# Row halves transposed by DMA for a first FFN layer, and a new timetable of branch steps between gate products

## The reference

```python
x = x + jnp.tanh(g_xattn[0]) * wkv0(w, u, k=_layernorm(x), v=ctx)
x = x + jnp.tanh(g_ffn[0]) * ffn0(_layernorm(x))
x = x + jnp.tanh(g_xattn[1]) * wkv1(decay, first, k=_layernorm(x), v=ctx)
x = x + jnp.tanh(g_ffn[1]) * moe(_layernorm(x))
# ffn0: hidden = silu(x @ W1.T) * (x @ W3.T), 2048 wide; hidden = fwht(hidden); out = hidden @ W2.T
# wkv: y_t = (sum over s < t of decay * exp(k_s) v_s + exp(u + k_t) v_t) / (the same without v)
# moe: 8 experts of width 1024, two of them per row, silu(x @ w1.T) * (x @ w3.T) @ w2.T
```

## Time and profile before

| what | us |
|---|---|
| median of three runs (lowest, highest) | 1480.47 (1476.39, 1480.92) |
| the profiled execution | 1483.66 |
| its span | 1482.0 |
| PE busy in the span | 1244.8 (84%) |
| DVE busy | 726.9 (49%) |
| ACT busy | 504.1 (34%) |
| POOL busy | 201.2 (14%) |
| mean granted clock of PE | 0.935 |

### The profile page before, as it was taken

The page is one execution under the profiler, slowest core; times in us unless marked ns, Lnnn a source line. Parts: engine busy times, 40 slices in busy tenths (PEclk is TensorE's granted clock), DMA queues, the critical chain, the costliest instruction groups (busy, mean ns, idle before and its releaser), DMA issues. The chain is left out here.

```text
span 1482.0 us, 18672 instructions
## 1 busy us (share of the span) xinstructions
PE 1244.8 (84%) x5785; PEld 590.9 (40%) x5786; DVE 726.9 (49%) x1175; ACT 504.1 (34%) x671; POOL 201.2 (14%) x206
## 2 busy tenths in 40 slices
PE   1278899898998898988913199989999999999995
PEld 0143344444453344534413044434444444444442
DVE  6957966869677686795675211212122122221221
ACT  3337557476563665645432011111111111111110
POOL 0000000000002000030200413222222223222222
PEclk9989999999999999999955599999999999999998
DMA  6024576554756556637776278798959896955433
GB/s 253 29 114 136 178 248 220 171 191 171 254 166 85 181 197 219 214 95 260 213 204 208 46 182 160 146 121 179 186 138 189 178 201 134 163 120 100 77 67 61
DMA packets 228347, 239.13 MB, mean 161 GB/s; under 512 B 137168, under 2 KB 141520, under 8 KB 225168
## 3 DMA queue, kind: packets, MB, share of 16 engines
q1 hardware_dynamic: 84960, 164.58, 36.3%
q10 hardware_dynamic: 130368, 51.65, 20.4%
q0 software_dynamic: 12960, 22.15, 7.8%
...
## 5 line engine op out<-in xcount | busy, mean ns | idle before, releaser
L1084 PE MATMUL PS<-weights,xs 128*128 x1872 | 412.9, 381 | 29.5 <-DMA xs<-X 29.5
L1009 PE MATMUL PS<-xs,weights 128*128 128x512 f16 x1536 | 358.4, 390 | 26.8 <-DVE sg L845 15.1
L1084 PEld LDWEIGHTS PS<-weights,xs 128*128 128x128 f16 x1872 | 183.8, 98 | 252.3 <-issue 33.3
L1009 PEld LDWEIGHTS PS<-xs,weights 128*128 128x128 f16 x1536 | 152.6, 100 | 222.9 <-issue 24.2
L912 DVE SCALAR_TENSOR_TENSOR A<-A,PS 128x1024 f32<-128x1024 f32 x39 | 47.6, 1221 | 352.2 <-PE PS L1084 324.1
L1021 PE MATMUL PS<-weights,hs 128*128 128x512 f16 x768 | 181.3, 387 | 0.0
L604 ACT ACTIVATE A<-PS 128x1024 f32<-128x1024 f32 x39 | 39.9, 1024 | 320.1 <-PE PS L1084 192.2
...
L923 DVE TENSOR_SCALAR V<-PS,outl 128x512 f32<-128x512 f32 x39 | 29.3, 751 | 166.7 <-PE PS L1098 150.6
L1021 PEld LDWEIGHTS PS<-weights,hs 128*128 128x128 f16 x768 | 76.4, 100 | 86.2 <-issue 6.6
L1098 PE MATMUL PS<-weights,xs 128*128 x456 | 104.0, 386 | 7.9 <-DMA weights<-e 4.6
L612 ACT ACTIVATE E<-A 128x1024 f16<-128x1024 f32 x39 | 41.2, 1056 | 198.6 <-DVE A L912 156.0
...
## 6 DMA issues: line engine op xcount, KB each, us to landing
e<-halves SPq DMA_DIRECT2D x192, 256.0 KB
...
raw<-ew SPq DMA_DIRECT2D x119, 256.0 KB, 4.0
...
V<-ctx_cm ACTq DMA_DIRECT2D x7, 1024.0 KB, 5.7
X<-w ACTq DMA_DIRECT2D x4, 1024.0 KB, 6.1
out<-X ACTq DMA_DIRECT2D x4, 1024.0 KB, 9.9
...
```

The lines of the kernel that those rows point to most:

```text
L1009: ins = te.matmul(bank(bk), wj[:, j, w, a, c * P:(c + 1) * P], xs[:, g % 2, b, c, :], start=(k == 0 and c == 0), stop=(k == 2 and c == C - 1))
L1084: ins = te.matmul(bank(n), xTt[k][:, b, c, :], weights_of(off, 2 * I // NT * c + n, a), start=(c == 0 and m == 0), stop=(c == C - 1 and m ...
```

## The change

- STEPS has four places: ACT's and DVE's chunks are written anew. Place 2 is on ACT behind hh, place 3 on ACT and DVE at the chunk's end. DVE runs only places 0 and 3, ACT all; PE places 0 and 1 as before. Unit 0 stands behind silu on ACT and behind the gate product on DVE, all other units behind hh and place 2 (ACT) and behind hl (DVE). The residual moves from the head of chunk j = 1 to behind hl of chunk j = 0.
- In STEPS, exp, ln, norm and r2 are at place 2, the scans and the mix at place 3; yT0 is two chunks behind the mix's number. The branches' FIRST, GATES, UNITS and LATE have new numbers.
- The pre branches of groups 1 to 3 have no xT0 and xT1. xh copies the second norm's rows to the high half in `xr` (ACT), xl makes the low half (DVE), and the step xd issues four transposing DMAs from ACT, one per tile of 128 rows (128 x 1024 of float16), from `xr` into `xs`. PE waits for them (xs_in) at j = 0, and so does k0 ahead of its scans, since SQ is their source. Pre 0 in the prologue keeps its PE transposes.
- The bonus on the key sums moves from k1 and den into k0 and k1, and all scans of V into den.

```diff
 ADD, SUB, MUL, MAXO = ALU.add, ALU.subtract, ALU.mult, ALU.max
 
 
-UNITS = [[3, 3, 3, 3, 0, 3, 3, 3, 2, 3, 3, 3, 4, 4, 4, 2],
-         [3, 3, 3, 2, 4, 4, 4, 4, 2, 3, 4, 3, 2, 3, 3, 3],
-         [1, 1, 2, 1, 4, 3, 2, 4, 4, 4, 4, 2, 3, 4, 3, 2],
-         [4, 4, 4, 1, 4, 2, 0, 4, 3, 2, 4, 4, 4, 4, 4, 4]]
+UNITS = [[1, 2, 2, 3, 0, 1, 3, 3, 3, 1, 4, 4, 4, 3, 3, 4],
+         [3, 4, 4, 1, 4, 4, 4, 3, 3, 4, 4, 3, 3, 0, 3, 3],
+         [2, 3, 3, 4, 0, 4, 4, 1, 4, 4, 4, 3, 3, 4, 4, 4],
+         [0, 0, 4, 4, 4, 3, 3, 4, 0, 4, 4, 4, 4, 4, 4, 4]]
 assert sum(map(sum, UNITS)) == NU
 
 
 
-STEPS = [("stats", 0, 0), ("r0", 0, 0), ("newton", 0, 0), ("norm", 1, 0), ("kT0", 1, 1), ("e0", 2, 0), ("k0", 2, 0),
-         ("kT1", 2, 1), ("e1", 3, 0), ("k1", 3, 0), ("den", 4, 0), ("ln", 4, 1), ("rec", 4, 1), ("num", 5, 0), ("mix", 6, 0),
-         ("yT0", 6, 1), ("add0", 7, 0), ("yT1", 7, 1), ("add1", 8, 0), ("r2", 8, 0), ("newton2", 8, 0), ("norm2", 8, 1),
-         ("xT0", 9, 0), ("xh0", 9, 0), ("xl0", 9, 0), ("xT1", 9, 1), ("xh1", 10, 0), ("xl1", 10, 0), ("last", 10, 1),
-         ("raw", 11, 0)]
+
+
+STEPS = [("stats", 0, 0), ("r0", 0, 3), ("newton", 1, 0), ("norm", 1, 2), ("kT0", 2, 1), ("e0", 2, 2), ("k0", 2, 3),
+         ("kT1", 3, 1), ("e1", 3, 2), ("k1", 3, 3), ("ln", 4, 2), ("den", 4, 3), ("rec", 4, 3), ("num", 5, 3), ("mix", 6, 3),
+         ("yT0", 8, 0), ("add0", 8, 0), ("yT1", 8, 1), ("add1", 9, 0), ("r2", 9, 2), ("newton2", 9, 3), ("norm2", 10, 1),
...
+        "post": [("xT0", 11, 0), ("kt0", 11, 0), ("xl", 11, 0), ("xT1", 11, 1), ("kt1", 11, 2), ("last", 12, 0), ("raw", 12, 0)]}
+
+EARLY = {"stats": (1, 0), "r0": (1, 1), "newton": (1, 3), "norm": (1, 3)}
 BRANCHES = [("pre", 0), ("pre", 1), ("pre", 2), ("post", 0), ("pre", 3), ("post", 1), ("post", 2), ("post", 3)]
-FIRST = {("pre", 1): 0, ("pre", 2): 11, ("post", 0): 20, ("pre", 3): 30, ("post", 1): 39, ("post", 2): 49}
-GATE_STEPS = [("gate1", 0), ("gate1b", 0), ("gate2", 0), ("rank", 1), ("ranked", 0)]
-GATES = {0: (31, 32, 34, 34, 35), 1: (50, 51, 53, 53, 54), 2: (60, 61, 62, 61, 62)}
+FIRST = {("pre", 1): -1, ("pre", 2): 9, ("post", 0): 19, ("pre", 3): 29, ("post", 1): 39, ("post", 2): 49}
+GATE_STEPS = [("gate1", 0), ("gate1b", 0), ("rank", 1), ("gate2", 0), ("ranked", 0)]
...
             "xl1", ("h", 3)]
 QORDER = [u for k, u in (x for x in PROLOGUE if isinstance(x, tuple)) if k == "q"]
 
-LATE = {1: 2, 2: 3, 4: 4, 7: 5, 9: 6, 10: 7}
-EPILOGUE = [("post", NG - 1, s) for s, _, _ in STEPS] + [("post", NG - 1, s) for s, _ in GATE_STEPS]
...
+    return sum(kind == "pre" and g > 0 for kind, g in BRANCHES[:b])
 
...
         half = lambda t, a: t[:, :].rearrange("p (c a t) -> p c a t", c=C, t=T)[:, :, a, :]
-        xr = SQ[:, :].bitcast(F16).rearrange("p (s i d) -> p s i d", s=2, i=TILES)
+        xr = SQ[:, :].bitcast(F16).rearrange("p (i s d) -> p i s d", i=TILES, s=2)
...
                     if not second and b >= 1:
-                        act.wait_ge(s["side_full"], FILLS.index(BRANCHES[b - 1] + ("xT1",)) + 1)
-                        act.wait_ge(s["xrl_done"], posts_before(b))
+                        if BRANCHES[b - 1] + ("xT1",) in FILLS:
+                            act.wait_ge(s["side_full"], FILLS.index(BRANCHES[b - 1] + ("xT1",)) + 1)
+                        if b >= 2:
+                            act.wait_ge(s["xrl_done"], b - 1)
...
+                elif step == "xh":
+                    act.wait_ge(s["norm_done"], n + 2)
+                    act.activation(xr[:, :, 0, :], four(A1[:, :]), ACT.Copy, scale=SX).then_inc(s["xrh_done"], 1)
+                elif step == "xd":
+
+                    act.wait_ge(s["xrh_done"], b)
+                    act.wait_ge(s["xrl_done"], b)
+                    if g >= 2:
+                        act.wait_ge(s["b_done"], J * (g - 1))
+                    for i in range(TILES):
+                        act.dma_start_transpose(xs[:, g % 2, :, :, i * P:(i + 1) * P].rearrange("p s c n -> p (s c) n"),
+                                                xr[:, i, :, :].rearrange("p s d -> p (s d)")).then_inc(s["xs_in"], 16)
-                    if kind == "pre":
-                        if a == 0 and g >= 2:
-                            act.wait_ge(s["b_done"], J * (g - 1))
-                        act.activation(xs[:, g % 2, 0, a:a + 2, :].rearrange("p c n -> p (c n)"), side, ACT.Copy, scale=SX).then_inc(s["xh_done"], 1)
-                    else:
-                        act.activation(ch(E1, a, 2), side, ACT.Copy).then_inc(s["kt_done"], 1)
-                        if a == 0:
-                            act.activation(xr[:, 0, :, :].rearrange("p i d -> p (i d)"), A1[:, :], ACT.Copy, scale=SX).then_inc(s["xrh_done"], 1)
-                        else:
-                            rows = xn_rows[g * NT:(g + 1) * NT, :].rearrange("(i p) (s d) -> s p i d", p=P, s=2)
-                            act.wait_ge(s["xrh_done"], g + 1)
-                            act.dma_start(rows[0], xr[:, 0, :, :]).then_inc(s["xn_out"], 16)
-                            act.wait_ge(s["xrl_done"], g + 1)
-                            act.dma_start(rows[1], xr[:, 1, :, :]).then_inc(s["xn_out"], 16)
+                    act.activation(xs[:, 0, 0, a:a + 2, :].rearrange("p c n -> p (c n)"), side, ACT.Copy, scale=SX).then_inc(s["xh_done"], 1)
+                elif step in ("kt0", "kt1"):
+                    a = 2 * int(step[2])
+                    act.wait_ge(s["side_full"], FILLS.index((kind, g, "xT" + step[2])) + 1)
+                    act.activation(ch(E1, a, 2), side, ACT.Copy).then_inc(s["kt_done"], 1)
+                    if a:
+                        rows = xn_rows[g * NT:(g + 1) * NT, :].rearrange("(i p) (s d) -> s p i d", p=P, s=2)
+                        act.wait_ge(s["xrh_done"], b)
+                        act.dma_start(rows[0], xr[:, :, 0, :]).then_inc(s["xn_out"], 16)
+                        act.wait_ge(s["xrl_done"], b)
+                        act.dma_start(rows[1], xr[:, :, 1, :]).then_inc(s["xn_out"], 16)
...
-                for u in units[0:1]:
-                    unit_high(u)
                 if n >= 2:
                     act.wait_ge(s["hl_done"], n - 1)
                 act.wait_ge(s["a_done"], n + 1)
                 act.activation(sg[:, n % 2, :], bank(ABANK), ACT.Silu, scale=1.0 / (SW * SX)).then_inc(s["sil1_done"], 1)
+                for u in units[0:1]:
+                    unit_high(u)
                 for step in steps_beside(g, j, 1):
                     run(*step)
-                for u in units[1:2]:
-                    unit_high(u)
                 if n >= 2:
                     act.wait_ge(s["down_done"], n - 1)
                 act.wait_ge(s["hid_done"], n + 1)
                 act.activation(hs[:, n % 2, 0, :], sg[:, n % 2, :], ACT.Copy).then_inc(s["hh_done"], 1)
-                for u in units[2:]:
+                for step in steps_beside(g, j, 2):
+                    run(*step)
+                for u in units[1:]:
                     unit_high(u)
+                for step in steps_beside(g, j, 3):
+                    run(*step)
...
+                    if pres_before(b):
+                        ve.wait_ge(s["xs_in"], 16 * TILES * pres_before(b))
                     scan(layer, SQ, E1, (0, 1))
+                    bonus(layer, E1, SQ, (0, 1))
                 elif step == "k1":
                     ve.wait_ge(s["e1_done"], 2 * b + 2)
                     link(ve.tensor_tensor(ch(V, 2, 2), ch(E1, 2, 2), ch(V, 2, 2), MUL))
                     scan(layer, SQ, E1, (2, 3))
-                    bonus(layer, E1, SQ, (0, 1))
+                    bonus(layer, E1, SQ, (2, 3)).then_inc(s["den_done"], 1)
                 elif step == "den":
-                    bonus(layer, E1, SQ, (2, 3)).then_inc(s["den_done"], 1)
-                    scan(layer, A1, V, (0, 1, 2))
+                    scan(layer, A1, V, range(C))
                 elif step == "num":
-                    scan(layer, A1, V, (3,))
...
+                elif step == "xl":
+                    ve.wait_ge(s["xrh_done"], b)
+                    ve.scalar_tensor_tensor(xr[:, :, 1, :], four(A1[:, :]), SX, xr[:, :, 0, :], MUL, SUB).then_inc(s["xrl_done"], 1)
...
-                for step in steps_beside(g, j, 0) + steps_beside(g, j, 1):
+                for step in steps_beside(g, j, 0):
                     run(*step)
                 if n in LATE:
                     w_low(LATE[n])
-                for u in units[0:1]:
-                    unit_low(u)
                 ve.wait_ge(s["sil1_done"], n + 1)
                 ve.wait_ge(s["b_done"], n + 1)
                 ve.scalar_tensor_tensor(sg[:, n % 2, :], sg[:, n % 2, :], SH / (SW * SX), bank(BBANK), MUL, MUL).then_inc(s["hid_done"], 1)
-                for u in units[1:2]:
+                for u in units[0:1]:
                     unit_low(u)
                 ve.wait_ge(s["hh_done"], n + 1)
```

(12 more changed lines are left out.)

27 lines of the change are left out of this document (14 added, 13 removed).

## The result

| | before | changed |
|---|---|---|
| median of 10 runs (lowest, highest), us | 1477.17 (1471.82, 1480.92) | 1485.35 (1482.6, 1489.69) |
| ratio, 95% interval | | 1.0059 [1.004, 1.0077] |
| the profiled execution, its span | 1483.66, 1482.0 | 1485.73, 1484.1 |
| first A product, end of the last down product | 113.3, 743.1 | 110.0, 752.0 |
| first stage between them | 629.8 | 642.0 |

The changed kernel is slower by 0.59%, 8.7 us on the median of before; the forecast was +7.5. The profiled spans differ by less, 2.1 us, because the experts' stage took 633.1 us in before's trace and 626.3 in this one; of that, one wait of PE for weights, 4.56 us at 996 us, is in before's trace alone, and the rest is not placed. Up to the last down product the changed kernel is 8.9 us behind: +12.2 in the first stage, -3.3 in the prologue. From there to the first slot's products both take 105.8 us.

The account below looks back on a forecast made before the run. PE was the fullest engine in the first stage, stalling on ACT and DVE. Stalls +15.7, transposes -5.2 and lower clock -3 gave net +7.5 us, put at 1488 us; range 1456 to 1510.

Parts of the forecast that it names:

- Stalls of the first stage: PE's waits in the first layer's 64 chunks: 75.3 us after the change, against 59.6 before, so +15.7.
- The chain (3): ACT and DVE steps within a branch: gate products 11.3, 11.3, 10.8, 8.2, 8.4 us apart; 12.8 us of stalls in two branches.
- 4.5 of slack: First-layer chunks: DVE's gate product may run 4.5 us behind before PE stalls; silu has as much.
- The transposing DMAs (4): Before pre 2, post 0 and post 1, four ACT issues delay the next norm, units and silu: 39.8 us of stalls together.
- X: Time ACT spends issuing four transposing DMAs: between 5.0 and 24 us, taken as 6.
- the late entry of DVE: DVE, waiting for units behind the issues, enters the branch 4 us late, turning 0.8 us of stall into 3.3.
- 3 more for post 1: Extra 3 us of stall for branch post 1, whose first chunk holds gate2 and ranked.
- The first branch (5): Pre 1, sharing chunks with w_high/w_low: three weight-load waits cost 8.7 us, on 14 of chain, together 22.7.
- The 14 put down for the chain itself: Share of the first branch's 22.7 us of stalls counted for its chain, apart from weight loads.
- The lower clock: PE's loss at the lower clock level is partly hidden once ACT and DVE are late: -3 us.
- Transposes: xT0 and xT1 before groups 1 to 3 leave PE: six times 0.87 us, -5.2 us.
- the waits simply go: Rival: waits for y and norm vanish in the first stage; -34 us in full, -25 halfway, to 1455; chance 0.33.

Follow-up runs that it names:

- e12: Changed kernel with ln issued behind its chunk's unit copies and rec behind the next chunk's; ratio to before 0.991, -22 us from changed.
- e1: Changed kernel with the four transposing DMAs issued at place 3 instead of 2, behind the unit copies; ratio to before 1.0005, -8 us from changed.
- e5: Changed kernel with GpSimd's row-list scatters held until the first layer's last down product; ratio to before 0.9978, -12 us from changed.
- e2: Changed kernel with the first layer's weight pieces loaded one piece earlier; ratio to before 1.0034, -4 us from changed.
- e6: Changed kernel with three edits together, e1, e2 and e5; ratio to before 0.9872, -28 us from changed.
- e8: e6 with group 0's last two gate steps, gate2 and ranked, also moved from chunk 41 to 39; ratio to before 0.9881, -26 us from changed.
- e9: The kernel before, with only the row-list scatters held until the last down product; ratio to before 0.9935, 9.6 us faster.
- e7: e8 with the transposes of token groups 1 to 3 back on TensorE instead of DMA; ratio to before 0.9872, -28 us from changed.

## Why the prediction was right, and where it was not

The sign and the main mechanism held: stalls moved from y to a chain of ACT and DVE. That the size came so near is in part luck: the first stage is 12.2 us longer, where +7.5 was worked out, and a prologue that the text does not name gave 3.3 back. By its terms:

- **Stalls of the first stage**: 75.3 worked out, 76.3 measured. By branch the agreement is poorer: pre 2, 13.4 against 13.3; post 0, 11.7 against 9.8; pre 3, 5.2 against 5.6; post 2, 7.6 against 8.6; but pre 1, 22.7 against 11.8, and post 1, 14.7 against 18.5, with 8.8 in chunk 60 that had no term. So the sum agrees because 10.9 too much in pre 1 stand against 12.6 too little in post 1 and chunk 60.
- **The chain (3)** was right in its spacings, and silu's stall behind ln and rec was 3.0 to 4.4 us five times, for 3.6. What the text did not see is that the chain stood there for one order of two steps: e12 takes out 22 us, more than the change cost. Slack was counted against PE, but not what DVE could have done while ACT computed ln. Two slips did no harm: for the third spacing, put at 10.8, the text's own terms give 11.2 (ln for the exps, one unit less, eight scans), which is what was measured; and the 7.7 us of lag before cannot be 4.5 of slack and then stalls, if 5.2 of them stood at yT0 (PE's stalls in that branch were 0.88 + 5.22).
- **The transposing DMAs (4)**: X was 6 and measured 6.42 to 6.52; kT0 waited 5.1 and 4.3 for 3.5, while the late entry of DVE cost less (1.9 and 0.4 for 3.3). X was worth 18 us in the sum, three times 3.5 + 2.5. e1 takes out 8 us, and with the scatters held e1 and e2 together give 15 (e5 to e6). The Trainium skill (VectorE: DVE Perf Modes, section "The three transpose paths") gives 1309 ns for a 128 x 128 transpose by DMA. The trace does not bear out the 42 us that the prediction estimated from it for 32 blocks: eight blocks land 3.2 to 5.6 us behind their issue, 4.1 in the median, the four DMAs overlap and are all down 8.3 to 8.5 us behind the first issue, and no row shows k0 waiting for SQ.
- **"3 more for post 1"** is the mis-sized term: kT0 waited 10.1 us in chunk 41. Gate2 and ranked are 3.4 us of small DVE instructions, but they stood behind units that had waited 8.9 us for ACT, itself behind the issues. e1 cut the wait to 3.9, so most of it was the issues' again; ranking in chunk 39 takes the 3.9 away (e6 to e8), and that much was the rank's.
- **The first branch (5)**: 22.7 was too much. Loads back to back were there (10.4 us of ACT), but most of it was slack; e2 got 3.2 us for the 8.7 counted. The 14 put down for the chain itself has no working in the text; in e2, without the loads' waits, PE stalls 10.0 us in this branch.
- **Chunk 60 (8.8 us) and the silu of chunk 43** were missing: they come from stores behind GpSimd's scatters, shown by e5, which takes out all of chunk 43's and 5.7 of the 8.8. The steps of the gate were moved in the change, and so were the scatters that they release, and this I did not follow to its DMA queue.
- **The lower clock**: -3 was the wrong sign. The time at the lower clock in the stage went from 54.6 to 64.9 us; its longest stretches, 10.2 us each, begin in the single stalls of 10.1 and 8.8 us. Stalls and transposes give +16.7 - 5.2 = +11.5 of the stage's +12.2, which leaves under 1 us for it.
- **The prologue**, which the text does not name, is 3.3 us shorter, and 3.0 of that is PE's clock. Before, PE waits 2.82 us for y, and from 73.0 to 79.9 us the granted clock is at its lower level (1.2 GHz); in the changed kernel PE waits 1.96 us, and the clock stays at 2.4 GHz. The same eight transposes and 32 products, before and then changed:

```profile
73.82 1.94 PE L986 MATMUL PS<-idn,V 128*128 128x128 f32 x8 [2.82 <-DVE V L723]
75.55 9.20 PE L1039 MATMUL PS<-weights,hads 128*128 128x512 f16 x32
```

```profile
73.47 1.07 PE L1010 MATMUL PS<-idn,V 128*128 128x128 f32 x8 [1.96 <-DVE V L748]
74.38 7.07 PE L1063 MATMUL PS<-weights,hads 128*128 128x512 f16 x32
```

(In e9, with the old order, the clock falls there too (from 73.9 us); in none of the twelve profiles with the new order does it.)

- **Transposes**, -5.2: in the sum with their full value, since PE seemed to bound the stage. e7 shows them hidden.
- **A rival's number**: *the waits simply go* had -34 in full and "halfway" -25; half is -17, which is 1463 and not 1455.

Of the lines on what would show it: waits for gate product and silu came to 35.6 (over 35), three waits for w loads were there, y fell below 8, the stage was over 620. At the same products 5.7 us of waits for add0 came in, which I had put at up to 1.9 per branch. The 3.7 us missed on the clock and the 3.3 of the prologue nearly cancel.
